# One layer of a vision tower on one core: a step of weighing moved behind a step of scores, and the second bias as one fp32r product over stacked halves

## The chip, the core and the metric

The kernel runs on one core of a Trainium2 chip. The metric is the device time of one execution in microseconds (us). A core has five engines that run side by side and meet at semaphores: TensorE (PE, matrix products; PEld is its loading of weights), VectorE (DVE), ScalarE (ACT), GpSimd (POOL) and SyncE (SP), which here only issues DMA. PE accumulates in PSUM, in banks of 128 partitions by 512 fp32 values.

## What is computed

The reference, cut to what matters:

```python
h = einsum('bhid,oi,od->bho', x, weighted_sum, weight)          # 8 batches of 512 tokens, 256 values each
h = h + attention(layernorm(h))                                  # 16 heads of 16, rotary, cosine scores, softmax
# attention: scores = q.k * SCALE; attn = softmax(scores); out = attn @ v; out @ out_w.T + out_b
x_flat = layernorm(h)
probs = sigmoid(x_flat @ Wg + bg);  weights = probs * (probs > 0.5)   # 8 experts
hid = relu(einsum('td,edh->eth', x_flat, W1) + b1)
expert_out = einsum('eth,ehd->etd', hid, W2) + b2
combined = einsum('te,etd->td', weights, expert_out)
h = h + combined
```

The term of the second bias is a product of its own, `weights @ b2` (512 tokens by 8 experts, times 8 by 256); it is kept near fp32 accuracy.

## The kernel before, in words

Eight batches of 512 tokens are done in turn. The work on a batch has two halves: attention (with mixing, norms, projections and gates) and the experts. The experts of one batch run interleaved with the attention of the next, so that there are: a first stage with the attention of batch 0 alone, a second body (experts of batch 0 with attention of batch 1, which also splits the expert weights into fp16 high and low parts), six merged bodies, and a last stage with the experts of batch 7 alone.

The expert work comes in 64 chunks (8 experts times 8 slices of the hidden layer). `f1 c` is the first product of a chunk: 6 fp16 products of 512 columns into `bank_h` (L850), after which ACT writes `h32` and `hh` (L657, L660) and POOL their difference `hl` (L540). `f2 c` is the second product, three chunks later: 12 fp16 products of 256 columns into `bank_f` (L869, L871, L872). After each expert DVE adds `bank_f` to the result (`acc`, L1073).

The attention work is put between these chunks by `attention_order`: each step has a place in time, in units of one chunk, and `merge` sorts the steps and puts each in the half chunk before `f2` or the one behind it. Every engine runs the same list of steps; `exps_first` lets ACT take a step of scores ahead of an `f1` that stands just before it. Steps that matter here:

- `scores n` (32 a batch): two products with 64 rows of contraction, 512 columns each, into `bank_s` (L767). ACT turns them into `probs` (L627).
- `weigh u` (16 a batch): four heads, each a fp32 product of `probs` with 32 columns of weights, into the four quarters of `bank_o` (L779; the hardware runs each as two records, so 8 per step). It needs the `probs` of scores 2u and 2u+1. Its place is behind scores 2u+3, by 0.1 of a chunk. With a pace of 0.66 chunks per step of scores, that 0.1 is sometimes across the edge of a half chunk, and then an `f1` or `f2` comes between.
- `out_copy g` and `out_turn g` (4 a batch) take `bank_o` away (ACT) and turn it (PE, L789).
- `gates` computes on DVE the weights of the experts, `wg` (L1038 to L1047), `gates_turn` turns them on PE (L827) and copies them on ACT into `wt`, which is 8 partitions of `tmp_a`, and `bias2` multiplies them with `b2sb`, 8 by 256, in fp32 (L833: four products, eight records), after which DVE adds the result (L1059). `gates_turn` stands behind `f1 63` and `bias2` behind `f2 60`, so that bias2 on PE waits for ACT's copy, and ACT's copy stands behind the two ACT instructions of chunk 63.

Of the kernel before, what the change touches and what calls it, by code (L numbers as in the profile page):

```python
# [18 lines left out]
F32 = mybir.dt.float32  # L19
F32R = mybir.dt.float32r  # L20
F16 = mybir.dt.float16
I32 = mybir.dt.int32
ALU = mybir.AluOpType
# [32 lines left out]
def attention_order(alone=False):  # L56
# [19 lines left out]
    for u in range(UNITS):  # L76
        steps.append((first + PACE * (2 * u + 3) + 0.1, "weigh", u))
# [115 lines left out]
def build(nc, x_t, mix_w, mix_sum_t, qkv_w_t, qkv_b, out_w_t, out_b, gate_w, gate_b, w1, b1_t, w2, b2,  # L193
# [5 lines left out]
    with ExitStack() as ctx:  # L199
        def sb(name, shape, dt=F32):  # L200
            return ctx.enter_context(nc.sbuf_tensor(name, shape, dt))
# [4 lines left out]
        def sem(name):  # L206
            return ctx.enter_context(nc.semaphore(name))
# [14 lines left out]
        b2sb = sb("b2sb", [EXPERTS, D])  # L222
# [47 lines left out]
        wt = tmp_a[0:EXPERTS, :]  # L270
# [27 lines left out]
        pool_consts = sem("pool_consts")  # L298
        mix_in = [sem(f"mix_in{i}") for i in range(2)]
# [136 lines left out]
        def _(sp):  # L436
# [18 lines left out]
            for dst, src in ((ident, unit), (qkvb, qkv_b.partition_broadcast(P)), (cos, rope_cos), (sin, rope_sin),  # L455
                             (outb, out_b.partition_broadcast(P)), (gatew, gate_w.rearrange("(k p) e -> p k e", p=P)),
                             (gateb, gate_b.partition_broadcast(P)), (b1raw, b1_t), (b2sb, b2)):
                sp.dma_start(dst[:], src).then_inc(consts_in, 16)
            load_x(0, [2, 3])
# [74 lines left out]
        def _(pool):  # L534
# [30 lines left out]
            pool.wait_ge(consts_in, 16 * 9)  # L565
# [4 lines left out]
        def _(act):  # L570
# [18 lines left out]
            def steps(stage, n, fb, ab):  # L589
# [60 lines left out]
                elif stage == "gates_turn":  # L650
                    wait(act, gturned, ab, 1)
                    copy(wt, bank_m[0:EXPERTS, :]).then_inc(gt_out.sem, 1)
# [24 lines left out]
        def _(pe):  # L677
# [17 lines left out]
            def steps(stage, n, fb, ab):  # L695
# [15 lines left out]
                elif stage == "ln1_turn":  # L711
# [8 lines left out]
                    if n == 0 and fb is None:  # L720
                        pe.wait_ge(consts_in, 16 * 9)
# [100 lines left out]
                elif stage == "gates_turn":  # L822
# [3 lines left out]
                    for t in range(TT):  # L826
                        last = pe.transpose(bank_m[0:EXPERTS, t * P:(t + 1) * P], wg[:, t, :], ident[:])  # L827
# [53 lines left out]
        def _(dve):  # L881
# [23 lines left out]
            def steps(stage, n, fb, ab):  # L905
# [26 lines left out]
                elif stage == "ln1":  # L932
                    wait(dve, mixed_out, ab, 2 * TT)
                    norm_scale(ab)
                    if fb is None:
                        dve.wait_ge(consts_in, 16 * 9)
# [99 lines left out]
                elif stage == "gates":  # L1036
# [8 lines left out]
                    wait(dve, gturned, ab, 0)  # L1045
                    flat = [z[:].rearrange("p t e -> p (t e)") for z in (wg, lg, pg)]
                    dve.scalar_tensor_tensor(flat[0], flat[1], 0.0, flat[2], ALU.is_gt, ALU.mult)\  # L1047
                       .then_inc(gweight.sem, 1)
                    wait(dve, gweight, ab, 1)
# [38 lines left out]
                elif stage == "parts":  # L1088
# [6 lines left out]
                    dve.scalar_tensor_tensor(low, cut, scale, high, ALU.mult, ALU.subtract).then_inc(parts_lo, 1)  # L1095

# [81 lines left out]
```

## Time and profile before

| | |
|---|---|
| median of 3 runs | 2010.56 us (2005.82, 2010.56, 2010.73) |
| the profiled execution: its time, its span | 2008.53 us, 2006.6 us |
| busy share of PE, ACT, DVE, POOL | 95%, 57%, 39%, 34% |
| mean granted clock of PE | 0.975 |

PE products are pipelined: the records of neighbouring products overlap, so the length of one record is not what it costs. What a product costs is read as the distance from its start to the start of the next. In the timelines a row is: start in us from the start of the span, length, engine, line, operation, output<-inputs, shapes, count; in brackets the idle time of the engine before it and what ended it.

### The profile page before, as it was taken

The numbers are of one execution on the slowest core, as the hardware profiler recorded it, in microseconds if no ns is written. First come the engines' busy times: TensorE is split into PE (matmuls) and PEld (weight loads), VectorE is DVE, ScalarE is ACT, GpSimd is POOL, SyncE is SP. The second block draws the span as 40 slices with busy tenths as digits, with TensorE's granted clock in tenths as the row PEclk, the third lists the DMA queues.
The fourth block names the chain that finished last, engine by engine and source line by source line (L and its number), as shares of the span: only waits on it lengthen the run. The fifth ranks groups of instructions, "written<-read, shape, count | busy, mean of one in ns | idle before, by whom it ended". The sixth has DMA issues, their size and how long they took to land.

```text
span 2006.6 us, 33214 instructions
## 1 busy us (share of the span) xinstructions
PE 1907.4 (95%) x13152; PEld 1210.5 (60%) x13152; DVE 776.4 (39%) x1636; ACT 1143.0 (57%) x1969; POOL 676.7 (34%) x570
## 2 busy tenths in 40 slices
PE   5679898899999999999999999999999999999999
PEld 4246543576547764577646775467645776466666
DVE  6656933538103470145502372034800455022000
ACT  2654676544774467644765447754576447654444
POOL 1102422335223343333423353233433334233443
PEclk8779999999999999999999999999999999999999
DMA  4013232332112311231212221133211322113221
GB/s 156 31 57 113 104 138 84 126 138 84 64 64 106 115 64 64 79 125 63 83 64 105 97 84 64 64 106 97 83 64 64 124 77 85 64 64 116 101 89 53
DMA packets 40442, 176.64 MB, mean 88 GB/s; under 512 B 4056, under 2 KB 17120, under 8 KB 23904
## 3 DMA queue, kind: packets, MB, share of 16 engines
q1 hardware_dynamic: 40288, 174.52, 24.8%
q8 instruction: 105, 1.72, 0.3%
q14 instruction: 49, 0.40, 0.1%
HBM read 153.54 MB, written 20.97 MB: 87 GB/s over the span
## 4 chain that ended last, share of the span: by engine, by line
PE 78%; DVE 8%; issue 6%; ACT 1%; POOL 1%; POOLq 0%; DVEq 0%; ACTq 0%
PE bank_h L850 28%; PE bank_f L869 10%; PE bank_f L871 10%; PE bank_f L872 10%; PE bank_o L779 5%; PE bank_s L767 3%; PE bank_s L683 2%; PE bank_s L685 2%; PE bank_s L684 2%; PE bank_s L752 1%; DVE qk L972 1%; DVE tmp_b L967 1%; DVE y L890 1%; POOL hl L540 1%; PE bank_s L833 1%
## 5 line engine op out<-in xcount | busy, mean ns | idle before, releaser
L540 POOL TENSOR_TENSOR hl<-h,hh 128x512 f16<-128x512 f32 x512 | 608.2, 1188 | 1131.8 <-ACT hh L660 724.9
L850 PE MATMUL bank_h<-x,w1s 128*128 128x512 f16 x3072 | 754.8, 383 | 9.0 <-ACT hh L660 8.6
L657 ACT ACTIVATE h<-bank_h,b1s 128x512 f32<-128x512 f32 x512 | 353.6, 691 | 453.3 <-PE bank_h L850 438.3
L869 PE MATMUL bank_f<-w2s,hh 128*128 128x256 f16 x2048 | 562.3, 275 | 2.1 <-DVE acc L1073 1.6
L871 PE MATMUL bank_f<-w2s,hh 128*128 128x256 f16 x2048 | 560.5, 274 | 0.0
L872 PE MATMUL bank_f<-w2s,hl 128*128 128x256 f16 x2048 | 560.4, 274 | 0.0
L850 PEld LDWEIGHTS bank_h<-x,w1s 128*128 128x128 f16 x3072 | 288.2, 99 | 333.9 <-issue 43.5
L660 ACT ACTIVATE hh<-bank_h,b1s 128x512 f16<-128x512 f32 x512 | 352.6, 689 | 0.0
L627 ACT ACTIVATE probs<-bank_s 128x512 f32<-128x512 f32 x480 | 262.4, 604 | 154.6 <-PE bank_s L767 154.2
L869 PEld LDWEIGHTS bank_f<-w2s,hh 128*128 128x128 f16 x2048 | 201.9, 99 | 112.5 <-issue 43.0
L1073 DVE SCALAR_TENSOR_TENSOR acc<-bank_f,gw,acc 128x256 f32<-128x256 f32 x256 | 106.1, 477 | 364.0 <-PE bank_f L872 363.9
L871 PEld LDWEIGHTS bank_f<-w2s,hh 128*128 128x128 f16 x2048 | 201.3, 98 | 48.1 <-issue 0.3
L872 PEld LDWEIGHTS bank_f<-w2s,hl 128*128 128x128 f16 x2048 | 201.2, 98 | 24.1
L1000 DVE RECIPROCAL rc<-bank_m 128x16 f32<-128x16 f32 x32 | 8.2, 258 | 400.0 <-PE bank_m L789 400.0
L779 PE MATMUL bank_o<-probs,v 128*32 128x512 f32 x1024 | 138.1, 612 | 1.2 <-ACT tmp_b L572 0.6
L767 PE MATMUL bank_s<-qt,kt 64*128 64x512 f16 x480 | 99.2, 393 | 13.0 <-ACT probs L627 11.8
L683 PE MATMUL bank_s<-mix,xh 128*128 128x256 f32 x256 | 77.9, 304 | 15.9 <-DVE xl L913 15.9
L767 PEld LDWEIGHTS bank_s<-qt,kt 64*128 64x128 f16 x480 | 24.6, 93 | 100.0 <-issue 49.7
L609 ACT ACTIVATE probs<-qk 128x512 f32<-128x512 f32 x32 | 20.2, 630 | 102.9 <-DVE qk L954 102.9
L913 DVE TENSOR_TENSOR xl<-xraw,xh 128x512 fp32r<-128x512 f32 x64 | 47.7, 757 | 76.0 <-ACT xh L572 63.6
L684 PE MATMUL bank_s<-mix,xh 128*128 128x256 f32 x256 | 73.7, 288 | 0.0
L685 PE MATMUL bank_s<-mix,xl 128*128 128x256 f32 x256 | 73.5, 287 | 0.0
(134 smaller groups left out, 1736.0 us busy)
## 6 DMA issues: line engine op xcount, KB each, us to landing
w1s<-w_parts SPq DMA_DIRECT2D x56, 1024.0 KB, 4.8
w2s<-w_parts SPq DMA_DIRECT2D x56, 1024.0 KB, 4.8
xraw<-in_x_t_dram SPq DMA_DIRECT2D x32, 512.0 KB, 4.8
raw<-in_w_dram SPq DMA_DIRECT2D x16, 1024.0 KB, 6.7
w_parts<-w1s SPq DMA_DIRECT2D x8, 1024.0 KB, 8.8
w_parts<-w2s SPq DMA_DIRECT2D x8, 1024.0 KB, 10.7
out_dram<-acc SPq DMA_DIRECT2D x16, 256.0 KB, 6.1
raw<-in_qkv_w_t_dram SPq DMA_DIRECT2D x1, 768.0 KB, 7.2
```

The costliest lines, as they stand in the source:

```text
L540: pool.tensor_tensor(hl[n % HBUFS][:], h32[n % 2][:], hh[n % HBUFS][:], ALU.subtract)\
L627: act.activation(probs[u % 2][:, 2 * half + j, :], score_bank(2 * n + j, fb is None)[:, :], ACT.Exp, scale=SCORE_SCALE).then_inc(exped.sem, 1)
L657: act.activation(h32[n % 2][:], bank_h[n % 2][:, :], ACT.Relu, bias=b1s[:, e, m:m + 1]).then_inc(h_hi.sem, 1)
L660: act.activation(hh[n % HBUFS][:], bank_h[n % 2][:, :], ACT.Relu, bias=b1s[:, e, m:m + 1]).then_inc(h_hi.sem, 1)
L683: pe.matmul(out_ap, high[k], w[k], start=start and k == 0, stop=False, skip_group_check=True)
L684: pe.matmul(out_ap, high[k], lo_w[k], start=False, stop=False, skip_group_check=True)
L767: pe.matmul(score_bank(2 * n + j, fb is None)[:, :], kt[lo:lo + 64, h // 2, tile * P:(tile + 1) * P], qt[lo:lo + 64, h // 2, :], start=Tru ...
L779: last = pe.matmul(bank_o[32 * j:32 * j + 32, :], v1[:, tile, h, :, :].rearrange("p s d -> p (s d)"), probs[n % 2][:, j, :], start=(tile = ...
L850: last = pe.matmul(bank_h[n % 2][:, :], w[:, wp, k, m * P:(m + 1) * P], x16s[fb % 2][:, xp, k, :], start=(k == 0 and wp + xp == 0), stop=( ...
L869: pe.matmul(o, high, w[:, 0, m, :], start=(m == 0 and t % 2 == 0), stop=False, skip_group_check=True)
L871: pe.matmul(o, high, w[:, 1, m, :], start=False, stop=False, skip_group_check=True)
L872: last = pe.matmul(o, low, w[:, 0, m, :], start=False, stop=(m == HM - 1), skip_group_check=True)
```

## The change

Two edits. First, `weigh u` stands exactly behind scores 2u+3 (the 0.1 becomes 0.000001), and the last one, whose place would lie behind scores 33, is put at place 32. Second, the gates times the second bias: `wg` is split into a high part that fp32r holds exactly and a low rest, and laid out as high, low, high (`wg3`, 24 columns); `b2` is loaded three times one under the other and made once into high, high, low (`stack_b2`, in batch 0). One fp32r product over 24 rows then gives the three partial products that matter. `wt` becomes a tile of its own.

```diff
-        steps.append((first + PACE * (2 * u + 3) + 0.1, "weigh", u))
+        steps.append((first + PACE * min(2 * u + 3, 2 * UNITS) + 1e-6, "weigh", u))
...
-        b2sb = sb("b2sb", [EXPERTS, D])
+        b2raw = sb("b2raw", [3 * EXPERTS, D])
+        b2sb = sb("b2sb", [3 * EXPERTS, D], F32R)
+        b2low = sb("b2low", [3 * EXPERTS, 1])
...
-        wt = tmp_a[0:EXPERTS, :]
+        wg3 = sb("wg3", [P, TT, 3, EXPERTS], F32R)
+        wt = sb("wt", [3 * EXPERTS, TOKENS], F32R)
...
-                             (gateb, gate_b.partition_broadcast(P)), (b1raw, b1_t), (b2sb, b2)):
+                             (gateb, gate_b.partition_broadcast(P)), (b1raw, b1_t)):
                 sp.dma_start(dst[:], src).then_inc(consts_in, 16)
+            for part in range(3):
+                sp.dma_start(b2raw[part * EXPERTS:(part + 1) * EXPERTS], b2).then_inc(b2_in, 16)
...
-            pool.wait_ge(consts_in, 16 * 9)
+            pool.wait_ge(consts_in, 16 * 8)
...
                 elif stage == "gates_turn":
                     wait(act, gturned, ab, 1)
-                    copy(wt, bank_m[0:EXPERTS, :]).then_inc(gt_out.sem, 1)
+                    wait(act, b2_done, ab, 0)
+                    copy(wt[:], bank_m[0:3 * EXPERTS, :]).then_inc(gt_out.sem, 1)
...
-                        last = pe.transpose(bank_m[0:EXPERTS, t * P:(t + 1) * P], wg[:, t, :], ident[:])
+                        last = pe.transpose(bank_m[0:3 * EXPERTS, t * P:(t + 1) * P],
+                                            wg3[:, t].rearrange("p s e -> p (s e)").bitcast(F32), ident[:])
...
                     wait(dve, gturned, ab, 0)
+                    if ab == 0:
+                        stack_b2()
                     flat = [z[:].rearrange("p t e -> p (t e)") for z in (wg, lg, pg)]
-                    dve.scalar_tensor_tensor(flat[0], flat[1], 0.0, flat[2], ALU.is_gt, ALU.mult)\
+                    att_v.link(dve, dve.scalar_tensor_tensor(flat[0], flat[1], 0.0, flat[2], ALU.is_gt, ALU.mult))
+                    dve.tensor_copy(wg3[:, :, 0, :], wg[:])
+                    att_v.link(dve, dve.tensor_copy(wg3[:, :, 2, :], wg[:]))
+                    dve.tensor_tensor(wg3[:, :, 1, :], wg[:], wg3[:, :, 0, :].bitcast(F32), ALU.subtract)\
                        .then_inc(gweight.sem, 1)
-                    wait(dve, gweight, ab, 1)
...
+            def stack_b2():
+
+                dve.wait_ge(b2_in, 16 * 3)
+                dve.wait_ge(consts_in, 16 * 8)
+                b2_made.link(dve, dve.tensor_copy(b2sb[:], b2raw[:]))
+                dve.tensor_reduce(b2low[:], ident[0:3 * EXPERTS, 2 * EXPERTS:3 * EXPERTS], AX.X, ALU.add)
+                b2_made.link(dve, dve.scalar_tensor_tensor(b2raw[:], b2sb[:].bitcast(F32), -2.0, b2raw[:],
+                                                           ALU.mult, ALU.add))
+                b2_made.link(dve, dve.scalar_tensor_tensor(b2sb[:], b2raw[:], b2low[:], b2sb[:].bitcast(F32),
+                                                           ALU.mult, ALU.add))
```

How the rows move. On PE, in the first merged body, at `weigh 1` (L779 before, L787 after): L767 or L775 is a step of scores, L850 or L859 is `f1 29`, L869 to L872 or L878 to L881 are `f2`. Before:

```order
L872 MATMUL bank_f1<-w2s1,hl1 128x256
L767 MATMUL bank_s0<-qt,kt 128x512
L767 MATMUL bank_s1<-qt,kt 128x512
L850 MATMUL bank_h1<-x16_1,w1s1 128x512 x6
L779 MATMUL bank_o<-probs1,v1 32x512 x4
L869 MATMUL bank_f0<-w2s1,hh2 128x256
L871 MATMUL bank_f0<-w2s1,hh2 128x256
```

After:

```order
L881 MATMUL bank_f1<-w2s1,hl1 128x256
L775 MATMUL bank_s0<-qt,kt 128x512
L775 MATMUL bank_s1<-qt,kt 128x512
L787 MATMUL bank_o<-probs1,v1 32x512 x4
L859 MATMUL bank_h1<-x16_1,w1s1 128x512 x6
L878 MATMUL bank_f0<-w2s1,hh2 128x256
L880 MATMUL bank_f0<-w2s1,hh2 128x256
```

The weighing has moved ahead of `f1 29`. In every merged body, and in the second body too, `weigh 9` and `weigh 12` move ahead of the `f2` that stood between them and their scores, and `weigh 15` moves ahead of `f1 47`, from behind that chunk to behind `f2 43`. The other steps of weighing keep their place on PE. No other engine has work in a step of weighing, and none of their lists changes by this edit.

On DVE, in the gates of batch 0, from the reciprocal to the adding of the bias term. Before:

```order
L1044 RECIPROCAL pg<-pg 128x32
L1047 SCALAR_TENSOR_TENSOR wg<-lg,pg 128x32
L1051 COPY gw0<-wg 128x32
L1059 TENSOR_TENSOR acc0<-bank_s0,acc0 128x512
L1059 TENSOR_TENSOR acc0<-bank_s1,acc0 128x512
```

After:

```order
L1053 RECIPROCAL pg<-pg 128x32
L1114 CAST b2sb<-b2raw 24x256
L1115 TENSOR_REDUCE b2low<-ident 24x1
L1116 SCALAR_TENSOR_TENSOR b2raw<-b2sb,b2raw 24x256
L1118 SCALAR_TENSOR_TENSOR b2sb<-b2raw,b2low,b2sb 24x256
L1058 SCALAR_TENSOR_TENSOR wg<-lg,pg 128x32
L1059 CAST wg3<-wg 128x4x8
L1060 CAST wg3<-wg 128x4x8
L1061 TENSOR_TENSOR wg3<-wg,wg3 128x4x8
L1064 COPY gw0<-wg 128x32
L1072 TENSOR_TENSOR acc0<-bank_s0,acc0 128x512
```

Four instructions now stand ahead of `wg` in batch 0 alone, and three behind it in every batch, before PE may turn the gates.

## Rows read from the trace of the kernel before

**Rows 1.** The page: PE's granted clock in 40 slices, in tenths.

```profile
PEclk8779999999999999999999999999999999999999
```

**Rows 2.** Busy time by stretch: us, then PE, PEld, DVE, ACT, POOL, clock, DMA.

```profile
300.00:360.00 60.00, 52.06 (x309) 24.02 (x311) 20.05 (x35) 38.94 (x65) 14.01 (x13) 0.89 0.26 88
412.00:647.00 235.00, 233.04 (x1646) 148.16 (x1645) 86.22 (x188) 138.50 (x242) 83.25 (x69) 1.00 0.24 84
...
1587.00:1822.00 235.00, 232.82 (x1645) 148.06 (x1644) 86.10 (x187) 138.49 (x242) 83.36 (x69) 1.00 0.23 79
```

**Rows 3.** Timeline of PE around weigh 1 and weigh 2 of a merged body.

```profile
528.04 0.39 PE L767 MATMUL bank_s<-qt,kt 64*128 64x512 f16 x2
528.36 1.47 PE L850 MATMUL bank_h<-x,w1s 128*128 128x512 f16 x6
529.76 1.07 PE L779 MATMUL bank_o<-probs,v 128*32 128x512 f32 x8
530.76 0.28 PE L869 MATMUL bank_f<-w2s,hh 128*128 128x256 f16 x1
...
534.22 1.06 PE L779 MATMUL bank_o<-probs,v 128*32 128x512 f32 x8
535.21 0.28 PE L869 MATMUL bank_f<-w2s,hh 128*128 128x256 f16 x1
...
536.95 1.47 PE L850 MATMUL bank_h<-x,w1s 128*128 128x512 f16 x6
538.26 0.27 PE L869 MATMUL bank_f<-w2s,hh 128*128 128x256 f16 x1
```

**Rows 4.** Timeline of PE at the end of an f2, then weigh 12.

```profile
588.73 0.27 PE L871 MATMUL bank_f<-w2s,hh 128*128 128x256 f16 x1
588.84 0.27 PE L872 MATMUL bank_f<-w2s,hl 128*128 128x256 f16 x1
589.04 1.07 PE L779 MATMUL bank_o<-probs,v 128*32 128x512 f32 x8
```

**Rows 5.** Timeline of ACT: the exponentials of scores 31, the last that weigh 15 needs.

```profile
599.84 1.09 ACT L627 ACTIVATE probs<-bank_s 128x512 f32<-128x512 f32 x2 [0.73 <-PE bank_s L767]
```

**Rows 6.** Timeline around bias2 of a merged body, ACT and PE.

```profile
654.03 0.57 ACT L572 ACTIVATE tmp_a<-bank_m 8x512 f32<-8x512 f32 x1
...
654.31 0.27 PE L872 MATMUL bank_f<-w2s,hl 128*128 128x256 f16 x1
654.65 1.99 PE L833 MATMUL bank_s<-b2sb,tmp_a 8*128 8x256 f32 x8
656.58 0.28 PE L869 MATMUL bank_f<-w2s,hh 128*128 128x256 f16 x1
```

**Rows 7.** Timeline of PE in the mixing: fp32r products of 256 columns.

```profile
666.11 0.28 PE L684 MATMUL bank_s<-mix,xh 128*128 128x256 f32 x1
666.23 0.28 PE L685 MATMUL bank_s<-mix,xl 128*128 128x256 f32 x1
```

**Rows 8.** Timeline of DVE, POOL and PE at the gates of a merged body.

```profile
650.26 0.19 DVE L1047 SCALAR_TENSOR_TENSOR wg<-lg,pg 128x32 f32<-128x32 f32 x1
650.49 0.19 DVE L1053 TENSOR_TENSOR gw<-wg,unscale 128x32 f32<-128x32 f32 x1
...
651.62 1.15 POOL L540 TENSOR_TENSOR hl<-h,hh 128x512 f16<-128x512 f32 x1 [1.81 <-PE bank_f L872]
...
652.67 0.60 PE L827 MATMUL bank_m<-ident,wg 128*8 128x128 f32 x4
```

**Rows 9.** Timeline at the gates and bias2 of batch 0, run alone.

```profile
139.32 1.15 POOL L540 TENSOR_TENSOR hl<-h,hh 128x512 f16<-128x512 f32 x1 [0.34 <-ACT hh L660]
139.44 1.08 DVE L1047 SCALAR_TENSOR_TENSOR wg<-lg,pg 128x32 f32<-128x32 f32 x1
...
140.57 1.02 PE L827 MATMUL bank_m<-ident,wg 128*8 128x128 f32 x4 [2.64 <-DVE wg L1047]
...
142.27 3.78 PE L833 MATMUL bank_s<-b2sb,tmp_a 8*128 8x256 f32 x8 [0.68 <-ACT tmp_a L572]
...
145.98 2.74 PE L850 MATMUL bank_h<-x,w1s 128*128 128x512 f16 x6
```

More of the change, by code:

```diff
@@ L298, in build @@
         pool_consts = sem("pool_consts")
+        b2_in = sem("b2_in")
+        b2_made = Chain(sem("b2_made"))
         mix_in = [sem(f"mix_in{i}") for i in range(2)]
@@ L720, in steps @@
                     if n == 0 and fb is None:
-                        pe.wait_ge(consts_in, 16 * 9)
+                        pe.wait_ge(consts_in, 16 * 8)
                     turn(ln1_turned, n, lambda k: normed[:, n, k * P:(k + 1) * P])
@@ L935, in steps @@
                     if fb is None:
-                        dve.wait_ge(consts_in, 16 * 9)
+                        dve.wait_ge(consts_in, 16 * 8)
                     wait(dve, ln2_turned, ab, 0)
@@ L1095, in steps @@
                     dve.scalar_tensor_tensor(low, cut, scale, high, ALU.mult, ALU.subtract).then_inc(parts_lo, 1)
+            def stack_b2():
+                dve.wait_ge(b2_in, 16 * 3)
+                dve.wait_ge(consts_in, 16 * 8)
+                b2_made.link(dve, dve.tensor_copy(b2sb[:], b2raw[:]))
[4 more added lines that the diff above has]
+                                                           ALU.mult, ALU.add))
             def make_scales(e):
```

## The prediction, as written before the run

> **What bounds the kernel now.** I read the clock first, then the busy time by stretch, then PE's timeline at the places that the change touches. The clock is at 7 or 8 tenths in the first three slices of 50 us [rows 1], still 0.89 between 300 and 360 us, and 1.00 in the merged bodies [rows 2]. The stretches [rows 2] show two kinds of time. A merged body takes 235.0 us, and PE is busy for 233.04 of them (232.82 in the last one): all six are PE's alone, and what PE is spared there comes off the end, as long as nothing else becomes late. In the second body PE is not always busy (52.06 us of 60 between 300 and 360, at a clock of 0.89): it stalls there behind the splitting of the weights, and a gain ahead of such a stall may be swallowed by it. So each edit is costed in a merged body as the distance between starts on PE, and the start-up is handled apart.
>
> **Weighing, what a move is worth.** PE's timeline shows a price for the edge between a full product (128 rows, 128 columns) and one that uses part of the array. Inside f2 the products start every 0.11 us, but the weighing starts 0.20 us behind the last of them [rows 4]: 0.09 for the edge. An f1 followed by f2 takes 1.31 us (536.95 to 538.26), one followed by a weighing takes 1.40 us (528.36 to 529.76) [rows 3]: again 0.09. Scores are such part products themselves, and the two of one step take 0.32 us with their edge (528.04 to 528.36); the weighing takes 1.00 us with its edge out (529.76 to 530.76; 534.22 to 535.21), whether a chunk or scores stand ahead of it [rows 3]. So where something full stands between scores and weighing there are two edges in, and one of them goes when they are neighbours.
>
> Weigh 1: before, 0.32 + 1.40 + 1.00; now 0.32 + 1.00 + 1.31. That is 0.09 us. Weigh 9 and 12: an f2 no longer ends with an edge, 0.09 each; I round each of the three to 0.10, since the first product behind a part product also starts about 0.01 late. Weigh 15 only changes an edge behind f1 for one behind f2 (it does not come to stand behind scores): nothing. A body gains 0.30, six bodies 1.8 us. In the second body the same three moves are worth 0.3 if no stall swallows them, and I count half, 0.15. In batch 0 nothing moves.
>
> What could wait now: weigh 15 starts some 1.3 us sooner, at about 602.1 instead of 603.4 on the scale of this body. Its last input are the exponentials of scores 31, which end at 599.84 + 1.09 = 600.93 [rows 5], 1.1 us ahead. Weigh 1, 9 and 12 need scores two steps older. The chunk that is now behind a weighing gets to ACT 1.0 us later in the two places where it is an f1 (29 and 47); ACT is busy for 138.5 of 235 us [rows 2] and has room, so I take nothing for it. Ends: 0 (if the edge does not go away when scores and a weighing are neighbours but is only paid elsewhere) to 2.3 us.
>
> **The bias product, merged bodies.** Before, from the first of the eight records to the next f2 it is 656.58 - 654.65 = 1.93 us, and ahead of it PE stands idle from 654.42 (0.11 behind the last f2) to 654.65, that is 0.23, for ACT's copy, which ends at 654.03 + 0.57 = 654.60 [rows 6]. That wait stays: the copy has 24 partitions in place of 8 and the same 512 columns, and stands behind the same work. Of the 1.93, an edge in and an edge out are about 0.10 + 0.09; the rest is 8 times 0.217. After, there are four records. What one costs on 24 rows no row of before shows. Upper bound: 0.217, as the fp32 records, so 4 x 0.217 + 0.19 = 1.06 and a gain of 0.87. Nearest row: fp32r products of the same 256 columns in the mixing start every 0.12 us (666.11 to 666.23) [rows 7]. I take that, since width and type are the same and only the number of rows differs: 4 x 0.12 + 0.19 = 0.67, a gain of 1.26. Lower bound: the f16 spacing of 0.11 without edges, 0.44, a gain of 1.49. Over the bodies that hold the bias of batches 1 to 7 (batch 1's stands at the end of the second body, behind its stalls) it is 7 x 1.26 = 8.8 us, between 6.1 and 10.4.
>
> **What the gates cost on DVE.** Turning the gates now waits for three more instructions. Linked DVE instructions on 32 values start 0.23 apart (650.26 to 650.49) [rows 8]. The two casts start at 650.49 and about 650.65, the subtraction at about 650.9, and it ends near 651.1. PE turns the gates at 652.67, behind f1 63. So 1.5 us of cover hide it, and the cost is nothing. The turning itself stays four products, with 24 columns of weights in place of 8.
>
> **Batch 0.** Here there is no cover. Before, PE waited 2.64 us for the gates [rows 9]. Ahead of them now stand stack_b2's four instructions, then the three. The first cast would start at 139.44, where L1047 started, and like it meet POOL's subtraction, which runs to 140.47: L1047 took 1.08 us there against 0.19 in the merged body [rows 8, 9]. I let the cast end at 140.8, give the reduction and two passes over 256 values 1.2 us together, the gates' own four 0.23 each: the gates are ready near 142.8 instead of 140.5, 2.2 us later. Against it stands the product: at half clock it took 145.98 - 142.27 = 3.71 us [rows 9], and half the records and half of each record make it about 1.3, a gain of 2.4. The sum is -0.2; I take 0, between +2 (the two passes slower, or a clock that comes back later for the longer idle time) and -2.
>
> **Loads.** SP issues two more small loads, ahead of an x tile that waits for something else; POOL, DVE and PE wait for one constant less. Nothing.
>
> **The sum**, against the profiled execution: 2008.53 - 8.8 - 1.8 - 0.15 + 0 = 1997.8. The median of the three runs, 2010.56, is 2.0 above that execution and the lowest of them 2.7 below; the mean of the four times is 2008.9, and against that the forecast is 1998.2 us.
>
> **Rivals.** (a) The gates are late after all. If the subtraction of the gates comes only after POOL's subtraction has started at 651.62, it is shut out until 652.77, ends near 653.0, and PE turns the gates at 653.05 instead of 652.67: 0.38 a body, 7 times 2.7 us, time 2000.9. For it: L1047 in batch 0, stretched to 1.08 us while POOL subtracted [rows 9]. Against: 0.5 us between the end I expect and 651.62. Two unlinked casts that were 0.3 slower each would decide it. The Trainium skill names this mechanism (SBUF — State Buffer, "Who interferes with whom"): a DVE instruction with two SBUF inputs, or a copy or cast that uses both ports, contends with GpSimd for a shared pair that is locked for a whole instruction. By that rule both casts and the subtraction are open to it, and the trace's stretched L1047, which has two such inputs, agrees. Chance of (a): 0.12.
>
> (b) A fp32r record on 24 rows costs what a fp32 record on 8 rows does: 7 x 0.87 = 6.1 in place of 8.8, time 2000.9. For it: nothing but that no row has this form. Chance 0.10.
>
> (c) The edges are not saved: the weighings are worth 0, time 2000.2. For it: scores and weighing divide the array in different ways, 64 rows against 32 columns, so that their neighbourhood may be an edge as well; against: weigh 2, behind scores, starts as soon and takes as long (1.00) as weigh 1 behind a chunk. Chance 0.08.
>
> (d) Slower than before. The one mechanism is the clock of the start. PE's idle time in batch 0 grows from 2.6 to about 4.9 us in a stretch whose clock is already below full, and the second body has a clock below full too (0.89 between 300 and 360) [rows 2]. Each us at half clock costs half a us of PE's work. To eat 10.7 us it takes over 21 us more at half clock than before, and for slower by 0.3% (6 us) 33 more. The spread of the three runs, 4.9 us, shows how much the start varies. A shift of 3 to 5 us either way is likely enough, a loss of all the gain is not: time 2012 or more, chance 0.03. That the same mechanism costs or gives some 4 us and leaves 2002 or 1994: chance 0.12 together.
>
> The forecast itself keeps 0.55.
>
> **How the numbers follow.** Predicted 1998.2. The bounds of the terms reach from 1998.2 - 1.6 - 0.5 - 2 = 1994 to 1998.2 + 2.7 + 1.8 + 2 = 2004.7 if all fell together; with the rivals at 2000 to 2002 and the spread of the start, 1994.5 to 2003.0 holds 8 in 10. About 0.3%, 6.0 us, is what a measurement of this kernel can tell from no change: faster means under 2004.5. That holds for the forecast, for (a), (b), (c) alone and for most of the shifts of the clock: 0.89. Within 0.3%: two rivals together with a bad start, 0.09. Slower by more: 0.02.
>
> **What would show it.** The merged body takes 235.0 - 1.26 - 0.30 = 233.4 us. From the first bias record to the next f2 it is 0.67 us, with the wait for ACT's copy still 0.23. Scores to weighing 0.32 and weighing to the next chunk 1.00 at weigh 1, 9 and 12. No new wait of PE for the gates in a merged body; one of about 4.9 us in batch 0. A body of 234.7 means that the bias gave nothing; 233.8 means rival (a) or (b), told apart by whether PE waits at the turning. If a body is 233.4 and the whole time still not below 2003, the start has lost it.

## The result, and the profile after the change

| | before | changed |
|---|---|---|
| median | 2011.11 us (2005.82 to 2016.69, 8 runs) | 2002.63 us (1999.41 to 2003.63, 8 runs) |
| the profiled execution: its time, its span | 2008.53, 2006.6 us | 2003.1, 2001.2 us |
| mean granted clock of PE | 0.975 | 0.974 |

The ratio is 0.9955, with a 95% interval of 0.9942 to 0.9968: the change takes 9.1 us off, between 6.4 and 11.7. The forecast was 10.7 us off, to 1998.2. The time is inside the range (1994.5 to 2003.0), at its upper end.

The windows view of the changed kernel, cut at the logits of the batches (what the prediction calls a body is the window from one batch's logits to the next one's; the rows of 1410.32 and 1401.03 us hold the six merged bodies). Columns as in [rows 2]. First the kernel before, in the same cut:

```profile
133.90:412.63 278.73, 244.54 (x1562) 148.41 (x1561) 156.73 (x285) 163.18 (x265) 85.42 (x72) 0.92 0.32 114
412.63:1822.95 1410.32, 1398.38 (x9866) 889.22 (x9865) 516.77 (x1123) 830.96 (x1453) 499.52 (x414) 1.00 0.24 83
1822.95:2006.60 183.65, 179.86 (x1248) 122.18 (x1246) 18.27 (x43) 85.10 (x136) 77.36 (x67) 1.00 0.25 87
```

Then the changed one:

```profile
0.00:135.65 135.65, 84.69 (x481) 51.83 (x482) 84.23 (x187) 63.65 (x117) 13.66 (x17) 0.80 0.26 89
135.65:417.77 282.12, 245.96 (x1558) 148.79 (x1557) 158.39 (x292) 163.35 (x265) 84.87 (x72) 0.91 0.32 113
417.77:1818.80 1401.03, 1389.33 (x9843) 886.04 (x9842) 518.77 (x1142) 831.69 (x1453) 499.35 (x414) 1.00 0.24 83
1818.80:2001.20 182.40, 178.51 (x1244) 121.26 (x1241) 18.57 (x46) 85.02 (x136) 77.42 (x67) 1.00 0.25 87
```

At full clock the change gives what was forecast: the six merged bodies are 9.29 us shorter and the last stage, which holds the bias of batch 7, 1.25. The 10.5 us together are more than the 5.4 by which the two spans differ. The second body is 3.4 us longer, and batch 0's logits come 1.75 us later. Where those 5.1 us come from is taken up below, where weigh 15 is put back and under "The start".

Weigh 1 in the changed kernel, PE's timeline; it answers to [rows 3]:

```profile
531.81 0.27 PE L881 MATMUL bank_f<-w2s,hl 128*128 128x256 f16 x1
532.01 0.39 PE L775 MATMUL bank_s<-qt,kt 64*128 64x512 f16 x2
532.33 1.06 PE L787 MATMUL bank_o<-probs,v 128*32 128x512 f32 x8
533.33 1.47 PE L859 MATMUL bank_h<-x,w1s 128*128 128x512 f16 x6
534.64 0.27 PE L878 MATMUL bank_f<-w2s,hh 128*128 128x256 f16 x1
```

The differences of the first column are 0.32, 1.00 and 1.31, as written beforehand; before they were 0.32, 1.40 and 1.00, in another order.

The gates and the bias product of the same body, DVE, POOL and PE; this answers to [rows 6] and [rows 8]:

```profile
654.11 0.18 DVE L1059 CAST wg<-wg 128x32 fp32r<-128x32 f32 x1
654.20 0.17 DVE L1060 CAST wg<-wg 128x32 fp32r<-128x32 f32 x1
654.41 0.19 DVE L1061 TENSOR_TENSOR wg<-wg 128x32 fp32r<-128x32 f32 x1
...
655.24 1.15 POOL L547 TENSOR_TENSOR hl<-h,hh 128x512 f16<-128x512 f32 x1 [1.81 <-PE bank_f L881]
656.30 0.60 PE L835 MATMUL bank_m<-ident,wg 128*24 128x128 f32 x4
...
657.93 0.27 PE L881 MATMUL bank_f<-w2s,hl 128*128 128x256 f16 x1
658.27 0.72 PE L842 MATMUL bank_s<-b2sb,wt 24*128 24x256 f32 x4
658.93 0.28 PE L878 MATMUL bank_f<-w2s,hh 128*128 128x256 f16 x1
```

The subtraction ends at 654.60, 1.7 us before PE turns the gates, and PE's row has no bracket: no wait. From the first bias record to the next f2 it is 0.66 us (forecast 0.67, before 1.93). The second record starts 0.222 us behind the first, the other two 0.113 behind the one before, and the next f2 0.204 behind the last. So the records are spaced like other fp32r products of 256 columns (0.12) and not like fp32 ones (0.217), and about 0.2 stays for the two edges. The wait for ACT's copy is still there: 0.34 from the last f2 to the first bias record, 0.23 more than between two f2.

Batch 0, where nothing covers the gates; it answers to [rows 9]:

```profile
141.59 1.17 DVE L1116 SCALAR_TENSOR_TENSOR b2raw<-b2sb,b2raw 24x256 f32<-24x256 f32 x1
142.79 0.47 DVE L1118 SCALAR_TENSOR_TENSOR b2sb<-b2raw,b2low,b2sb 24x256 fp32r<-24x256 f32 x1
143.30 0.19 DVE L1058 SCALAR_TENSOR_TENSOR wg<-lg,pg 128x32 f32<-128x32 f32 x1
...
144.07 1.03 PE L835 MATMUL bank_m<-ident,wg 128*24 128x128 f32 x4 [4.16 <-DVE wg L1061]
145.78 1.22 PE L842 MATMUL bank_s<-b2sb,wt 24*128 24x256 f32 x4 [0.68 <-ACT wt L579]
146.93 2.31 PE L859 MATMUL bank_h<-x,w1s 128*128 128x512 f16 x5
```

PE waits 4.16 us for the gates (before 2.64, forecast 4.9), and the product takes 1.15 in place of 3.71. From batch 0's logits on DVE to the product behind the bias it was 12.08 us, and is 11.28: the gates come 1.75 us later, the product is 2.56 us shorter.

### The profile page after: what moved, and what is told of

Same layout as the page of the kernel before. It is cut to its first block, busy times and chain, and to the rows that moved or that the text cites. A ratio compares the mean times of both kernels' runs of the same rounds, so it can differ in the third digit from the quotient of the medians.

```text
span 2001.2 us, 33188 instructions
## 1 busy us (share of the span) xinstructions
PE 1898.5 (95%) x13120; PEld 1207.9 (60%) x13120; DVE 780.0 (39%) x1664; ACT 1143.7 (57%) x1969; POOL 675.3 (34%) x570
## 4 chain that ended last, share of the span: by engine, by line
PE 78%; DVE 8%; issue 6%; ACT 2%; POOL 1%; POOLq 0%; DVEq 0%; ACTq 0%
PE bank_h L859 29%; PE bank_f L878 10%; PE bank_f L880 10%; PE bank_f L881 10%; PE bank_o L787 5%; PE bank_s L775 3%; PE bank_s L691 3%; PE bank_s L692 2%; PE bank_s L693 2%; PE bank_s L760 1%; DVE qk L981 1%; DVE tmp_b L976 1%; DVE y L899 1%; POOL hl L547 1%; PE bank_s L827 1%
## 5 line engine op out<-in xcount | busy, mean ns | idle before, releaser
L859 PE MATMUL bank_h<-x,w1s 128*128 128x512 f16 x3072 | 757.6, 384 | 9.1 <-ACT hh L668 8.6
L878 PE MATMUL bank_f<-w2s,hh 128*128 128x256 f16 x2048 | 562.8, 275 | 1.9 <-DVE acc L1086 1.2
L881 PE MATMUL bank_f<-w2s,hl 128*128 128x256 f16 x2048 | 561.1, 274 | 0.0
L859 PEld LDWEIGHTS bank_h<-x,w1s 128*128 128x128 f16 x3072 | 288.9, 99 | 339.1 <-ACT hh L668 45.5
L878 PEld LDWEIGHTS bank_f<-w2s,hh 128*128 128x128 f16 x2048 | 202.1, 99 | 109.7 <-issue 42.8
L881 PEld LDWEIGHTS bank_f<-w2s,hl 128*128 128x128 f16 x2048 | 201.4, 98 | 24.2
L787 PE MATMUL bank_o<-probs,v 128*32 128x512 f32 x1024 | 137.2, 608 | 1.8 <-ACT probs L634 1.2
L775 PE MATMUL bank_s<-qt,kt 64*128 64x512 f16 x480 | 98.7, 392 | 13.6 <-ACT probs L634 12.3
L775 PEld LDWEIGHTS bank_s<-qt,kt 64*128 64x128 f16 x480 | 24.4, 93 | 100.0 <-issue 49.9
```

The costliest lines, as they stand in the source:

```text
L775: pe.matmul(score_bank(2 * n + j, fb is None)[:, :], kt[lo:lo + 64, h // 2, tile * P:(tile + 1) * P], qt[lo:lo + 64, h // 2, :], start=Tru ...
L787: last = pe.matmul(bank_o[32 * j:32 * j + 32, :], v1[:, tile, h, :, :].rearrange("p s d -> p (s d)"), probs[n % 2][:, j, :], start=(tile = ...
L859: last = pe.matmul(bank_h[n % 2][:, :], w[:, wp, k, m * P:(m + 1) * P], x16s[fb % 2][:, xp, k, :], start=(k == 0 and wp + xp == 0), stop=( ...
L878: pe.matmul(o, high, w[:, 0, m, :], start=(m == 0 and t % 2 == 0), stop=False, skip_group_check=True)
L881: last = pe.matmul(o, low, w[:, 0, m, :], start=False, stop=(m == HM - 1), skip_group_check=True)
```

## The experiments

Each run has a profile, so a merged body is read to about 0.02 us in every one, while a whole time has a spread of 4 us and more. The bodies therefore decide on the mechanisms, and the whole times on what they come to. For reference: a merged body took 235.02 us before (the last one 235.24) and 233.49 after.

**The weighings alone**, on the kernel before:

```diff
-        steps.append((first + PACE * (2 * u + 3) + 0.1, "weigh", u))
+        steps.append((first + PACE * min(2 * u + 3, 2 * UNITS) + 1e-6, "weigh", u))
```

> The weighing alone, the bias product as before. Theory: the array's edges. A merged body of 235.02 us becomes 234.75 (the whole change gave 233.49, of which the bias product's own distance, 1.93 to 0.66 us, is 1.27, which leaves 0.26). Whole time 1 to 2 us below before, within the spread of the start. Rival: the weighing gives nothing and the bias all of 1.53: a body of 235.0. In the second body, theory: PE waits some 0.6 us for exponentials at weigh 15, as in the whole change; rival, that this wait came from the shifted bias work: no such wait.

Bodies of 234.60, 234.61, 234.81, 234.85, 234.60, 234.60: 0.42 us off in four of them, forecast 0.30. Compared step by step with the body before, weigh 1, weigh 9 and weigh 12 give 0.11 each, and out_turn behind weigh 12, a full product that now follows an f2 rather than a part product, gives another 0.05. Weigh 15 gives nothing. That is 0.36 to 0.38; the other 0.03 to 0.06 lies ahead of weigh 1, among products that this edit leaves as they were. The whole time was 2009.33 us (11 runs), ratio 0.9996 (0.9986 to 1.0005): by whole times alone this half of the change could not be told from none, though 2.3 us come off the six bodies (two of them were 234.81 and 234.85).

**The bias product alone:** the changed kernel with the old line for the weighings.

```diff
-        steps.append((first + PACE * min(2 * u + 3, 2 * UNITS) + 1e-6, "weigh", u))
+        steps.append((first + PACE * (2 * u + 3) + 0.1, "weigh", u))
```

> The bias product alone, the weighing in its old places. Theory: a merged body of 235.02 - 1.27 = 233.75 us, whole time 7 to 9 us below before, and no wait of PE at weigh 15 in the second body. Rival, weighing gives nothing: a body of 233.49. In batch 0 the first product behind the bias starts 0.8 us sooner, measured from the logits, as in the whole change.

2003.01 us, ratio 0.9961 (0.9948 to 0.9974). The bodies are 233.85 to 234.09. At the product itself 1.27 us is won, but by the end of the body only 1.17: 0.04 is given back across the mixing and 0.06 more across the products for q, k and v. Those are fp32r products that the change does not touch. So the weighings' 0.42 and the product's 1.27 would make 1.69, and the whole made 1.53: 0.10 of the missing 0.16 is this slowing of other products, and some 0.05 is what the run with the weighings alone won ahead of weigh 1.

**Where the 0.16 went: the new tiles behind all others.** The tiles wg3, wt, b2raw and b2low are declared last, so that every old tile has the place in the order of declarations that it had before; b2sb grows only in partitions.

```diff
-        b2raw = sb("b2raw", [3 * EXPERTS, D])
         b2sb = sb("b2sb", [3 * EXPERTS, D], F32R)
-        b2low = sb("b2low", [3 * EXPERTS, 1])
...
-        wg3 = sb("wg3", [P, TT, 3, EXPERTS], F32R)
-        wt = sb("wt", [3 * EXPERTS, TOKENS], F32R)
...
+        wg3 = sb("wg3", [P, TT, 3, EXPERTS], F32R)
+        wt = sb("wt", [3 * EXPERTS, TOKENS], F32R)
+        b2raw = sb("b2raw", [3 * EXPERTS, D])
+        b2low = sb("b2low", [3 * EXPERTS, 1])
```

> The whole change with its new tiles behind all others in SBUF, so that every tile of before has its old address. The whole change and the bias alone both run the fp32r products of the mixing 120 ns apart, the kernel before and the weighing alone 119 ns (means 119.8 against 118.8 over some 470 distances), and their merged body lacks 0.1 to 0.16 us of the two parts' sum. Theory: the addresses of the tiles; then the distance is 118.8 again and the body 233.49 - 0.15 = 233.35 us. Rival: it comes with the program or the chip's state after the fp32r bias product; then 119.8 and 233.49.

**The same from the other side: 28 bytes.** b2raw and b2low together move everything declared behind them by 1028 bytes in each partition, 4 more than a multiple of 32. Here a filler of 28 bytes follows b2low and is the only difference.

```diff
         b2low = sb("b2low", [3 * EXPERTS, 1])
+        sb("b2pad", [3 * EXPERTS, 7])
```

> The whole change with 28 unused bytes behind the flag tile b2low, whose 4 bytes shift all tiles behind it. With the new tiles last, the fp32r products of the mixing went from 119.8 back to 118.8 ns apart. Theory: the odd 4 bytes are the reason; then 118.8 with the new tiles where they are and the flag filled up to 32 bytes, body 233.35. Rival: where the tiles lie matters, not the 4 bytes: 119.8 and 233.49.

PE's timeline in the mixing, two rows that lie 22 starts apart, first of the changed kernel, then of the one with the tiles last, then of the one with the filler:

```profile
667.75 0.28 PE L692 MATMUL bank_s<-mix,xh 128*128 128x256 f32 x1
...
670.39 0.28 PE L693 MATMUL bank_s<-mix,xl 128*128 128x256 f32 x1
```

```profile
664.18 0.28 PE L692 MATMUL bank_s<-mix,xh 128*128 128x256 f32 x1
...
666.79 0.28 PE L693 MATMUL bank_s<-mix,xl 128*128 128x256 f32 x1
```

```profile
667.04 0.28 PE L693 MATMUL bank_s<-mix,xh 128*128 128x256 f32 x1
...
669.64 0.28 PE L694 MATMUL bank_s<-mix,xl 128*128 128x256 f32 x1
```

2.64, 2.61 and 2.60 us. Over all six bodies the mean distances, in ns, and the bodies, in us, are:

| | mixing | q, k, v, 256 columns | body |
|---|---|---|---|
| before | 118.96 | 118.6 | 235.02 |
| weighings alone | 118.76 | | 234.60 |
| changed | 119.8 | 119.7 | 233.49 |
| tiles last | 118.76 | | 233.33 to 233.38 |
| filler of 28 bytes | 117.56 | 116.97 | 233.08 to 233.41 |

The f16 products of the experts (216.6 and 109.5) are the same in all of them. Nothing but addresses differs between the last three kernels, so the spacing of fp32r products depends on where the tiles lie, by up to 2.8 ns in 119.7. The 0.2 between the first two rows comes without a new address and shows how far such a mean moves by itself; the second profile of the changed kernel gives 119.8 again. Tiles last wins back 0.13 of the 0.16. With the filler the mixing is faster than before the change, and a body up to 0.41 shorter. Neither expectation for the filler, 118.8 or 119.8, came true: a multiple of 32 does not bring back the old spacing, so the 4 bytes alone are not the rule. The tiles mix, qkvw and outw are declared ahead of every new tile, while xh, xl and the turned activations stand behind b2low; so the inputs that moved are the second kind. Which property of an address does it, these runs don't tell. The whole times, 1998.82 and 2001.11, are single ones.

**Are the casts safe from POOL?** The prediction's rival (a) was that the gates' DVE chain is shut out while POOL subtracts. In the merged body it ends too early for that. Here six more casts hold it up until POOL has started; the same values are written seven times.

```diff
-                    att_v.link(dve, dve.tensor_copy(wg3[:, :, 2, :], wg[:]))
+                    for _ in range(7):
+                        att_v.link(dve, dve.tensor_copy(wg3[:, :, 2, :], wg[:]))
```

> The whole change with the second cast of the gates done seven times, each linked to the next: 6 more DVE instructions of 0.23 us ahead of the subtraction, which moves it from 654.41 to about 655.8 on the scale of the first merged body, inside POOL's subtraction (655.24 to 656.39). Theory of the shared port: the casts and the subtraction that fall into that stretch are shut out, the subtraction ends at 656.6 or later and PE turns the gates 0.3 to 0.4 us late: a body of 233.8 to 233.9. Rival, no lock: the subtraction ends near 656.0, PE turns the gates at 656.30 as before, body 233.49.

```profile
656.03 2.44 DVE L1061 CAST wg<-wg 128x32 fp32r<-128x32 f32 x7
...
657.07 1.16 POOL L547 TENSOR_TENSOR hl<-h,hh 128x512 f16<-128x512 f32 x1 [1.81 <-PE bank_f L881]
...
658.51 0.19 DVE L1062 TENSOR_TENSOR wg<-wg 128x32 fp32r<-128x32 f32 x1
...
658.76 0.61 PE L835 MATMUL bank_m<-ident,wg 128*24 128x128 f32 x4 [0.47 <-DVE wg L1062]
```

Seven linked casts, each some 0.2 us from the next, would take 1.45; they took 2.44. One of the seven, started at 657.10, just behind POOL's start at 657.07, took 1.16 us; the other six took 0.17 to 0.18 each. The subtraction of the gates starts only after POOL has ended at 658.23, and PE waits 0.47 at the turning. Bodies 234.0 to 234.2 (expected 233.8 to 233.9), single time 2009.37. The rival's mechanism is real, and in the changed kernel it is kept off by the 0.64 us between the subtraction's end (654.60) and POOL's start (655.24). The Trainium skill (SBUF — State Buffer, "Who interferes with whom") says that a DVE copy or cast that uses both ports contends with GpSimd for a shared pair, locked for a whole instruction; the trace agrees, with 1 us for a cast of 0.18.

**Batch 0: the second bias made ready earlier.** stack_b2 moves into the time in which DVE waits for ACT's exponential (3.8 us in the changed kernel).

```diff
+                    if ab == 0:
+                        stack_b2()
                     wait(dve, gexp, ab, 1)
...
-                    if ab == 0:
-                        stack_b2()
```

> The whole change, with the stacking of b2 put where DVE waits 3.8 us for the exponential of batch 0. Theory: the 2.14 us that it took ahead of wg (141.16 to 143.30) go off PE's path, so PE's wait for the gates in batch 0 falls from 4.16 to about 2.0 us, and the distance from the logits to the first product behind the bias from 11.28 to about 9.3 us; whole time 1 to 2 us below the whole change. Rival: the clock of the start decides, and the time is within 0.5 us of the whole change or anywhere within 3. The merged body stays 233.49.

```profile
136.72 0.40 DVE L1116 SCALAR_TENSOR_TENSOR b2raw<-b2sb,b2raw 24x256 f32<-24x256 f32 x1
...
142.54 0.61 PE L835 MATMUL bank_m<-ident,wg 128*24 128x128 f32 x4 [1.47 <-DVE wg L1061]
```

PE's wait falls from 4.16 to 1.47, and logits to behind the bias from 11.28 to 8.55 us. L1116 takes 0.40 here against 1.17: it no longer meets POOL's subtraction. Of the 2.7 us in that distance 2.1 are the gates, as expected, and 0.6 is clock: the turning and the product ran at half clock in the changed kernel's profile and in part at full clock here. 2000.77 us, ratio 0.9950 (0.9935 to 0.9965), as against 0.9955 for the changed kernel: the 2.7 us are seen in the stage, and the whole times, whose intervals overlap, agree with them without showing them.

**The second body: weigh 15 put back behind f1 47.**

```diff
-        steps.append((first + PACE * min(2 * u + 3, 2 * UNITS) + 1e-6, "weigh", u))
+        steps.append((first + PACE * (2 * u + 3) + 1e-6, "weigh", u))
```

> The whole change, but weigh 15 stands behind f1 47 again. Theory: the wait of 0.63 us at weigh 15 in the second body goes, the merged body stays 233.49 within 0.02, since an edge behind f1 costs what one behind f2 does. Rival: weigh 15 behind f2 43 is itself part of the gain of 0.26 a body, and the body becomes 233.6.

In the changed kernel PE waits at weigh 15 of the second body:

```profile
360.23 0.27 PE L881 MATMUL bank_f<-w2s,hl 128*128 128x256 f16 x1
361.13 1.06 PE L787 MATMUL bank_o<-probs,v 128*32 128x512 f32 x8 [0.63 <-ACT probs L634]
```

0.90 from the f2 to the weighing in place of 0.20. ACT splits weights in this body (a pass of 1.15 us stands right ahead of these exponentials), so they end at 361.08, 0.05 before the weighing; in the first merged body they end at 604.53, 1.2 ahead of it. The wait is there in every other kernel that has weigh 15 behind f2 43, the weighings alone included (361.27 there), and gone with the weighing put back, where the merged bodies stay at 233.49 to 233.51. At its place it costs 0.7 us. The time, 2001.95, ratio 0.9955 (0.9938 to 0.9971), cannot show that little, and this profile's second body is still 280.01 us, 1.3 longer than before. What makes the rest is seen in the last stretch of the body, from PE's last long wait to the logits, in the kernel before, the changed one and the one with stack_b2 early, which holds the whole change (columns as in [rows 2]):

```profile
400.96:412.63 11.67, 11.67 (x86) 8.55 (x87) 5.02 (x13) 6.67 (x15) 3.47 (x3) 1.00 0.71 273
```

```profile
404.42:417.77 13.35, 13.35 (x86) 9.20 (x87) 4.97 (x13) 6.67 (x15) 3.47 (x3) 0.87 0.62 238
```

```profile
401.80:413.47 11.67, 11.67 (x86) 8.56 (x87) 5.02 (x12) 6.67 (x15) 3.47 (x3) 1.00 0.71 270
```

The same 86 products take 1.7 us more where 3.4 us at half clock fall among them. They do in nine of the fourteen profiles, this one and both of the changed kernel among them, and do not in the other five.

**Does the order of scores and weighing matter?** All weighings half a chunk later: no weighing stands directly behind a step of scores, ten stand directly ahead of one.

```diff
-        steps.append((first + PACE * min(2 * u + 3, 2 * UNITS) + 1e-6, "weigh", u))
+        steps.append((first + PACE * (2 * u + 3) + 0.5, "weigh", u))
```

> The whole change with each weighing half a chunk later: none stands directly behind its scores any more, but ten of the sixteen stand directly ahead of the next scores; fifteen of sixteen were neighbours of scores before. Theory A, an edge is paid wherever part and full products meet, whichever comes first: five edges more, 5 x 0.09 to 0.11 = 0.5 us, body 234.0. Theory B, only scores followed by a weighing save: fifteen times 0.1 = 1.5 us, body 235.0. Rival C: ACT's wait for the probs that a later weighing frees makes it worse than either, seen as new waits of PE for exponentials.

```profile
761.78 0.39 PE L775 MATMUL bank_s<-qt,kt 64*128 64x512 f16 x2
762.10 1.47 PE L859 MATMUL bank_h<-x,w1s 128*128 128x512 f16 x6
763.50 1.07 PE L787 MATMUL bank_o<-probs,v 128*32 128x512 f32 x8
764.50 0.39 PE L775 MATMUL bank_s<-qt,kt 64*128 64x512 f16 x2
764.82 0.28 PE L878 MATMUL bank_f<-w2s,hh 128*128 128x256 f16 x1
...
783.01 0.87 PE L775 MATMUL bank_s<-qt,kt 64*128 64x512 f16 x2 [0.62 <-ACT probs L634]
783.82 1.47 PE L859 MATMUL bank_h<-x,w1s 128*128 128x512 f16 x6
```

Weighing ahead of scores costs the same as behind: 1.00 and 0.32. So it is the number of changes between full and part products that counts, not their order. But the body is 235.3 to 235.5, 1.9 us longer, and edges explain 0.5 of it. The last two rows show what else: scores now wait for ACT, 3.7 us at six places of the merged bodies (none in the changed kernel), 0.62 a body, and from the waiting scores to the next f1 it is then 0.81 in place of 0.32. That is 1.1 more; 0.2 to 0.3 stays unexplained. The single time was 2013.05.

**The bias product over all 128 rows.** b2sb and wt get 128 partitions, the other 104 zero, so that the product is no part product; stack_b2 early.

```diff
-        b2sb = sb("b2sb", [3 * EXPERTS, D], F32R)
+        b2sb = sb("b2sb", [P, D], F32R)
...
-        wt = sb("wt", [3 * EXPERTS, TOKENS], F32R)
+        wt = sb("wt", [P, TOKENS], F32R)
```

> The whole change with b2 stacked early, as before, and the bias product over all 128 rows, where rows 24 to 127 of both operands are zero. Theory: the edges of the bias product, 0.11 in (658.275 to 658.497 against 0.113 between the others) and 0.09 out, go away, and four products of 0.12 follow each other: 0.48 to 0.52 us instead of 0.65, body 233.49 - 0.15 = 233.34. Rival: a part product has no edge of its own here, and the 0.22 is the start of fp32r behind fp16: then 0.6 and a body of 233.45.

```profile
653.53 0.27 PE L881 MATMUL bank_f<-w2s,hl 128*128 128x256 f16 x1
653.87 0.74 PE L842 MATMUL bank_s<-b2sb,wt 128*128 128x256 f32 x4
654.46 0.28 PE L878 MATMUL bank_f<-w2s,hh 128*128 128x256 f16 x1
```

From bias to f2 0.59 in place of 0.66. The edge out goes: from the last record to f2 it is 0.121 in place of 0.204. The 0.11 extra between the first and the second record stays (0.227, before 0.222), so behind a wait it is not an edge of the part product. The other records start 0.118 and 0.120 apart here in place of 0.113, but the rows are not shown to do it: this kernel has 0.113 as well, one body earlier, and 24-row records have 0.116 to 0.121 with the tiles last, with the filler, with the late gates, with all weighings half a chunk later and with the bias product one chunk later. Body 233.41 in four of six, 0.08 less, where 0.15 was expected; single time 1998.65.

**The bias product one chunk later**, so that ACT's copy is ready; stack_b2 early.

```diff
-                while waiting:
+                while waiting and (c > CHUNKS or waiting[0][1] != "bias2"):
...
-            while waiting and waiting[0][0] < c + 1:
+            while waiting and waiting[0][0] < c + 1 and (c < CHUNKS or waiting[0][1] != "bias2"):
```

> The whole change with b2 stacked early and bias2 behind f2 61 instead of f2 60. Theory: PE no longer waits 0.23 us for ACT's copy at the bias product (0.34 instead of 0.11 us from the last f2 to the first bias product), body 233.49 - 0.23 = 233.26. Rival: the next mixing waits for the addition of the bias term that much longer, body 233.49.

```profile
662.03 0.27 PE L881 MATMUL bank_f<-w2s,hl 128*128 128x256 f16 x1
662.24 0.73 PE L842 MATMUL bank_s<-b2sb,wt 24*128 24x256 f32 x4
662.90 0.28 PE L878 MATMUL bank_f<-w2s,hh 128*128 128x256 f16 x1
```

0.21 in place of 0.34 ahead of the product, and 0.66 behind its start as before: the wait of 0.23 was worth 0.13, since 0.10 of edge had been under it. Body 233.36 to 233.38 in five of six, where 233.26 was expected. The single time is 2005.38, in an execution with 109.4 us at half clock, the most of all profiles here, and says nothing of the edit.

**All of it together:** tiles last (without the filler), stack_b2 early, weigh 15 put back, the bias product over 128 rows and one chunk later. Beside it the changed kernel once more.

> All that helped, together: the whole change with the old tiles at their old addresses, b2 stacked early, the bias product over 128 rows, weigh 15 behind f1 47 again, and bias2 behind f2 61 instead of f2 60. Theory: a body of 233.49 less 0.13 (addresses), 0.08 (full rows) and 0.23 (no wait for ACT's copy) is 233.05 us, and 2 us less in batch 0, so 4 to 5 us below the whole change: 1997 to 1998 us in the median. Rival: the later bias term makes the next batch's first mixing wait, and the body stays at 233.3; or the start decides and the median is within 1.5 us of the whole change.

> The whole change, run again beside the kernel that joins what helped. Theory: merged bodies of 233.49 in this profile too, median 2001 to 2003 us, with the first split of x and the stretch from batch 0's gates to batch 1's (282.1 us before) scattered by some us: the loss of 3 us there in the first profile is spread of the start and not the change. Rival: the second body is 282 us again, 2 to 3 more than in the kernels without the moved weigh 15 or with early stacking, and so is owed to the change.

| | median | ratio to before | merged body | second body | at half clock |
|---|---|---|---|---|---|
| together | 1998.01 us (1991.48 to 2000.45, 6 runs) | 0.9933 (0.9916 to 0.9950) | 232.94 to 233.19 | 273.78 | 79.9 us |
| changed, again | 2001.77 us (1999.45 to 2004.07, 6 runs) | 0.9954 (0.9938 to 0.9970) | 233.48 to 233.51 | 282.32 | 93.1 us |

The kernel before stood at 2011.73 in these rounds. The combination is 13.7 us below it and 3.8 below the changed kernel; the intervals of the two ratios overlap. The merged bodies give 0.3 to 0.55 each of that, 2.6 us in all. That is more than the sum of the parts, 0.13 for the addresses, 0.08 for the full rows and 0.12 for the chunk. The bias product shows why:

```profile
650.22 0.27 PE L881 MATMUL bank_f<-w2s,hl 128*128 128x256 f16 x1
650.25 0.72 PE L842 MATMUL bank_s<-b2sb,wt 128*128 128x256 f32 x4
650.82 0.28 PE L878 MATMUL bank_f<-w2s,hh 128*128 128x256 f16 x1
```

From the f2 ahead of it to the f2 behind it is 0.58 to 0.59 us here, by unrounded starts (in the changed kernel 0.99, with the full rows alone 0.93, one chunk later alone 0.87). Without a wait and without a part product the extra 0.11 inside it and the edge ahead of it go as well; either of the two edits alone leaves the 0.11. The second body in the table is that of a profiled execution, the combination's fastest, with less time at half clock than any other; it must not be compared with the medians.

## Why the prediction was right, point by point

**The bound.** The merged bodies are PE's alone, as [rows 2] were read: their length fell with PE's work, and no new wait came up in them.

**The bias term, 1.26 a body.** It measured 1.27 at its place. The choice of the mixing's 0.12 rather than the fp32 record's 0.217 was right and slightly high in this kernel (0.113), so rival (b) fell. Keeping the wait of 0.23 was right as well.

**The weighing term, 0.30 a body.** It was too small: the run with the weighings alone gave 0.42, of which 0.37 at the moved steps. An edge with the late start behind it is 0.11 rather than 0.10, and the step that looked only at the three weighings missed out_turn, whose neighbour changed too, for 0.05. Rival (c) fell: scores and weighing are no edge to each other.

**What no step had: the addresses.** The step on the tiles priced instructions only. Every tile that a change adds moves those behind it, and here that took back 0.10 to 0.13 a body. By chance it cancels what the weighings gave beyond their term, and the body's 233.49 stands beside a forecast of 233.4 (235.0 less 1.56) with two errors in it.

**The gates' chain in a merged body, nothing.** Right: the subtraction ended 1.7 us ahead of PE, against 1.5 forecast. Rival (a) did not happen, but its mechanism did elsewhere: in batch 0, L1116 met POOL and took 1.17 in place of 0.40.

**Batch 0, -0.2, taken as 0.** It was -0.8 to the product behind the bias. The product behaved as forecast (1.15 against 1.3 us); the gates were late by 1.75 and not 2.2, so PE waited 4.16 and not 4.9. Little of it lasts: where PE next waits in both profiles, 47 and 67 us behind the logits, it is 0.2 us ahead of before, and at 136 us 0.1 behind. So the stalls of the second body swallow it, as the prediction feared for gains there, and nothing was near the truth after all.

**Second body, 0.15 won.** Wrong in sign. The step "what could wait now" checked weigh 15's input in a merged body, where the 1.1 us of room are real, and took it over for a body in which ACT also splits weights. There it became a wait that costs 0.7, more than the 0.3 of the other three moves.

**The start.** The 1.75 us at the first logits are not shown to be an effect of the change. The first split of x on ACT starts at 8.2 us in the profile before and between 9.4 and 10.5 in all thirteen others, the one that changes no load included, whose logits come at 136.0. With the weighing put back the split is late as well (10.2) and the logits come at 133.6, earlier than before. So this stage varies by 3 us between profiles.

Of the 3.4 us by which the second body is longer, 1.7 are the half-clock stretch in its last 13 us, 0.7 are weigh 15, and the other 1.0 is spread over the rest of it, which holds 3.9 us more at half clock than before (47.7 against 43.8). In the second profile of the changed kernel the body is as long, 282.32, with less time at half clock than before (40.8 us in all): there too 1.7 fall in the last stretch and 0.7 on weigh 15, and 2.3 lie between 136 and 177 us behind the logits, where it has a half-clock stretch of 3.4 us that the profile before has not, and a wait 0.7 longer. Half-clock time that it is spared elsewhere, next to PE's longest waits, gives back only about 1.2. So it counts where such a stretch falls, and not only how many there are. What puts them there, and whether the change has a part in it, is open; one profile of before is too little to say. Rival (d), in its mild form, is thus the likeliest reason for what is missing; as a loss of the whole gain it fell.

**The base.** The forecast was made against the mean of four times, 2008.9; the medians of before were 2011.11 to 2011.73 later on. Of the 4.4 us between 1998.2 and 2002.63, about 2.2 are this base. The other 2.2 are a gain of 8.5 between the medians against 10.7 forecast, which the interval of 6.4 to 11.7 does not tell apart.

## What to carry to other kernels

On a PE that is never idle, count the changes between full and part products along the queue, with all neighbours of the moved step: each cost about 0.1 us here, whatever the order. Take out a wait and an edge at the same product together: here the two gave 0.41 us, and 0.07 and 0.13 apart. When a moved step has slack in the steady body, look for the same step in the bodies where the engine that feeds it has other work. And try new small tiles behind the old ones before blaming the code for a per cent in the fp32r products.

## What the runs showed of the hardware

- The mean start-to-start distance of the q, k and v products, fp32r with 256 columns, was 116.97 ns in one kernel and 119.7 in another that differs from it in tile addresses alone; f16 products stayed at 216.6 and 109.5.
- A fp32r record of 256 columns over 24 rows starts 0.113 to 0.121 us after the one before, depending on the kernel, one over 128 rows 0.113 to 0.124, against 0.216 for an fp32 record over 8 rows.
- 86 products at the end of the second body took 11.67 us at full clock and 13.35 with 3.4 us of them at half clock.
- A DVE cast of 0.18 us and a DVE pass of 0.40 us became 1 us longer and 0.77 us longer when they met a POOL subtraction of 1.16 and 1.18 us.
- In several kernels some merged bodies are 0.23 us longer than their neighbours (234.81 and 234.85 among 234.60; 233.18 among 232.94; the last body of before). It appears where PE turns q and k, and its cause was not looked for further.
